# A post-norm decoder layer in 8-bit arithmetic: the order of a batch's maximum and the next batch's norm on VectorE

## The chip, the cores and the metric

The kernel runs on one core of a Trainium2 chip. The core has a matrix engine (TensorE, PE in the profile), a vector engine (VectorE, DVE), a scalar engine (ScalarE, ACT), GpSimd (POOL), and SyncE (SP), which here only issues transfers. Sixteen DMA engines move data between HBM and SBUF. The engines run their own instruction streams in order and meet through semaphores. The metric is the time of one execution on the device in microseconds, given as the median of several runs.

## The reference

The program computes three blocks of a decoder, each followed by a residual add and a layer norm: a self-attention whose activations and weights pass through power-of-two 8-bit quantisers, a cross-attention in f32, and a feed-forward block with quantised weights and a low-rank addition. x is (8, 512, 512), the context is (8, 512, 384), and there are 16 heads. What matters here is the start of the self-attention:

```python
def _pot_scale(x):
    m = jnp.maximum(jnp.max(jnp.abs(x)), 1e-08)
    return jnp.exp2(jnp.ceil(jnp.log2(m / INT8_MAX)))

mu = jnp.mean(x, axis=-1, keepdims=True)
var = jnp.var(x, axis=-1, keepdims=True)
h = (x - mu) * jax.lax.rsqrt(var + LN_EPS)
h = h * fq_round(ln_gamma) + fq_round(ln_beta)
qkv = fq_floor(fq_floor(h) @ fq_round(w_qkv))
```

The scale of fq_floor(h) is one number for all eight batches. It needs the largest absolute value of h over the whole tensor, so no value of h can be quantised before the last batch has been normed, and no product of h can start before that.

## The kernel before, in words

The work is cut into stages, each between places where all five engines meet. The change lies in the first stage (from the start to the first product with w_qkv, 0 to 153.16 us in the profiled execution). A batch is 512 tokens by 512 features; it is held as four tiles of 128 tokens.

For each batch b of the first stage:

- **SyncE** (lines 434 to 461) loads x of batch b into one of two buffers `xB[:, b % 2]` (1 MB) and the context into one of two buffers `cx[:, b % 2]`. For b + 2 it may only do so when the buffer is free: x waits for `z_turned` of batch b, the context for `kv_mm` of batch b. Then it waits for `h_ready` of batch b and stores h to `h_scr` (1 MB). All of these go down one queue in this order. ScalarE issues the loads of w_qkv and w_out (8.4 MB) on a queue of its own, once x of batches 0 and 1 is in (lines 1276 to 1280).
- **VectorE** runs `first_norm(b)` (lines 1601 to 1607): a wait for x, four `bn_stats` (L1573), four `bn_aggr` (L1579), twelve small steps for the reciprocal root (L1582 to L1590), and four 128x512 multiply-subtracts in place (L1598), each of which raises `z_ready`.
- **TensorE** turns the context (`turn_ctx`, L843, 12 transposes), then z (`turn_z`, L833, 16 transposes). `turn_z(b)` waits for `h_ready` of batch b - 1, since z of all batches is turned into the same four banks, and for `z_ready` of each tile.
- **ScalarE** takes the turned context out of its banks (L1294), then applies gamma and beta on the way out of the banks of z (`h_out`, L1288, four of 128x512), raises `h_ready`, and writes into one of two buffers `hB[:, b % 2]`. For b of 2 and more it first waits until h of batch b - 2 is stored and until its maximum is taken (`h_peak` at b - 1).
- **VectorE** runs `h_peak(b)` (lines 1618 to 1620): a wait for `h_ready` of batch b, then one reduction over 128x2048 (L1516 `stats<-arena`).

VectorE also does one-off work, put between the batches: the maximum of w_qkv and w_out (`weight_peaks`, b = 2, L1516 `peak<-arena`), their scales (b = 3), and their quantisation (L1633, L1634 at b = 3 and 4; L1637, L1638 at b = 5). After the maximum of the last batch it folds the eight maxima, GpSimd reduces over the partitions, VectorE makes the scale, SyncE's reload of h from `h_scr` must have landed, and `quantise_h` (L1665, L1669) makes the first operand of stage two, whose matmuls are L855.

The order on VectorE is the order in which the program text calls these functions; nothing reorders them. The loop of lines 1640 to 1654 writes it out.

Of the kernel before, what the change touches and what calls it, by code (L numbers as in the profile page):

```python
# [73 lines left out]
def decoder(nc, x, ctx_768, g_ln, b_ln, w_qkv, w_out, log_temp, Wq, bq, Wk, bk, Wv, bv, Wo, bo,  # L74
# [20 lines left out]
    with ExitStack() as ctx:  # L95
# [80 lines left out]
        def S(name):  # L176

            if name not in names:
                names[name] = sem(name)
            return names[name]  # L180
# [1324 lines left out]
        def _(dve):  # L1505
# [9 lines left out]
            def amax(dst, src, ax=AX.X):  # L1515
                return V.tensor_reduce(dst, src, ax, ALU.max, apply_absolute_value=True)  # L1516
# [75 lines left out]
            def norm_stats(ch, src):  # L1592

                norm_moments(ch, src)
                norm_factors(ch)

            def normed(dst, src, t):
                return V.tensor_scalar(dst, src, mv[:, t, 0:1], rstd[:, t:t + 1], ALU.subtract, ALU.mult)  # L1598


            def first_norm(b):
                ch = Chain(dve, S("norm_step"), NORM, b)
                dve.wait_ge(S(f"x_in{b % 2}"), 16 * (b // 2) + 16)
                norm_stats(ch, xB[:, b % 2])
                for t in range(NT):
                    normed(xB[:, b % 2, t, :], xB[:, b % 2, t, :], t).then_inc(S("z_ready"), 1)
                ch.end()

            def gamma_beta():
                dve.wait_ge(apeak_ready, 1)  # L1610
                power_of_two(S_GAMMA, S_BETA + 1)
                for n, (v, k) in enumerate(((gam, S_GAMMA), (bet, S_BETA))):
                    g8 = gam8[:, KC * n:KC * n + KC]
                    link(V.tensor_scalar(g8, v[:, :], iv(k), None, ALU.mult))
                    link(V.tensor_scalar(v[:, :], g8, sc(k), None, ALU.mult))
                dve.sem_inc(S("b16_ready"), 1)

            def h_peak(b):
                dve.wait_ge(S("h_ready"), b * KC + KC)
                amax(stats[:, b:b + 1], hB[:, b % 2], AX.XY).then_inc(S("h_peak"), 1)  # L1620

            def weight_peaks():
                dve.wait_ge(S("wA_in"), 16 * (KC + 1))
                link(amax(peak[:, S_WQKV:S_WQKV + 1], wqkv_f, AX.XY))
                link(amax(peak[:, S_WOUT:S_WOUT + 1], wout_f, AX.XY))
                dve.sem_inc(peak_ready, 1)

            def weight_scales():
                dve.wait_ge(apeak_ready, 2)
                power_of_two(S_WQKV, S_WOUT + 1)  # L1630

            def quantise_wqkv(k):
                link(V.tensor_scalar(w8[:, 0:3 * INNER], wqkv_f[:, k, :], iv(S_WQKV), None, ALU.mult))  # L1633
                link(V.tensor_copy(wqkv_q[:, k, :], w8[:, 0:3 * INNER]))  # L1634

            def quantise_wout():
                link(V.tensor_scalar(w8[:, :], wout_f.rearrange("p a b -> p (a b)"), iv(S_WOUT), None, ALU.mult))  # L1637
                link(V.tensor_copy(wout_q.rearrange("p a b -> p (a b)"), w8[:, :]))  # L1638

            first_norm(0)  # L1640
            gamma_beta()
            for b in range(NB - 1):
                h_peak(b)
                first_norm(b + 1)
                if b == 2:
                    weight_peaks()
                if b == 3:
                    weight_scales()
                if b in (3, 4):
                    quantise_wqkv(2 * b - 6)  # L1650
                    quantise_wqkv(2 * b - 5)
                if b == 5:
                    quantise_wout()
# [499 lines left out]
```

## Time and profile before

| | us |
|---|---|
| median of 3 runs | 2945.56 |
| lowest and highest of them | 2941.08, 2950.68 |
| the profiled execution, its own time | 2947.2 |
| its span, first to last instruction | 2945.4 |
| TensorE busy, VectorE busy, ScalarE busy | 2549.4, 2387.9, 1403.5 |
| first product of stage two starts at | 153.16 |

How to read the rows below. A row of the timeline has the start in us from the start of the span, the duration, the engine, the line, the operation with output and input, the count, and in brackets the idle time of this engine just ahead of it with what ended that idle time. A row of the waits has the engine and line that waited, what it waited for, the total in us, the times, and the longest. SPq and ACTq rows are transfers being issued, at their start. An issue row of the transfers has the size and the us from issue to landing; each such row comes from a stretch of time with that one issue in it. A row of a stretch of time has its bounds and length, then busy us and count of PE, PEld (weight loads), DVE, ACT and POOL, TensorE's granted clock as a share of 2.4 GHz, the DMA share, and GB/s.

### The profile page before, as it was taken

The numbers are of one execution on the slowest core, as the hardware profiler recorded it, in microseconds if no ns is written. First come the engines' busy times: TensorE is split into PE (matmuls) and PEld (weight loads), VectorE is DVE, ScalarE is ACT, GpSimd is POOL, SyncE is SP. The second block draws the span as 40 slices with busy tenths as digits, with TensorE's granted clock in tenths as the row PEclk, the third lists the DMA queues.
The fourth block names the chain that finished last, engine by engine and source line by source line (L and its number), as shares of the span: only waits on it lengthen the run. The fifth ranks groups of instructions, "written<-read, shape, count | busy, mean of one in ns | idle before, by whom it ended". The sixth has DMA issues, their size and how long they took to land.

```text
span 2945.4 us, 43234 instructions
## 1 busy us (share of the span) xinstructions
PE 2549.4 (87%) x13176; PEld 995.6 (34%) x13176; DVE 2387.9 (81%) x4130; ACT 1403.5 (48%) x2456; POOL 217.9 (7%) x210
## 2 busy tenths in 40 slices
PE   3299899969999957777769799999999999999997
PEld 3244322212222224444335222222223444444443
DVE  7889499999999969999889589988897755555554
ACT  2200233318998989999523155555555322221211
POOL 0000233310111110000000000111100000000000
PEclk7599999969998979999989899999999999999999
DMA  8342222214454543443216633443355510000000
GB/s 320 109 184 93 90 105 101 94 65 158 164 180 150 164 144 113 128 125 114 72 43 200 152 84 102 115 110 103 101 169 197 197 72 29 29 29 28 29 29 29
DMA packets 197749, 332.90 MB, mean 113 GB/s; under 512 B 32504, under 2 KB 118520, under 8 KB 187248
## 3 DMA queue, kind: packets, MB, share of 16 engines
q1 hardware_dynamic: 193312, 314.51, 33.2%
q10 hardware_dynamic: 4304, 16.78, 1.5%
q8 instruction: 63, 1.03, 0.1%
q14 instruction: 70, 0.57, 0.1%
HBM read 200.70 MB, written 130.51 MB: 112 GB/s over the span
## 4 chain that ended last, share of the span: by engine, by line
PE 53%; DVE 21%; issue 15%; ACT 7%; DMA 2%; DVEq 1%; SPq 0%; POOLq 0%; POOL 0%; ACTq 0%
PE bank L1068 9%; PE bank L1234 7%; PE bank L1223 7%; ACT arena L1329 6%; DVE stats L1516 6%; PE bank L1024 4%; DVE arena L1797 4%; PE bank L1032 4%; PE bank L1008 4%; PE bank L1122 3%; DVE arena L1812 3%; PE bank L915 2%; PE bank L923 1%; PE bank L1040 1%; PE bank L983 1%
## 5 line engine op out<-in xcount | busy, mean ns | idle before, releaser
L1516 DVE TENSOR_REDUCE stats<-bank 128x1024 f32 (+1 forms) x352 | 406.4, 1216 | 54.8 <-PE bank L892 32.4
L1329 ACT ACTIVATE arena<-arena 128x512 bf16<-128x512 int8 x512 | 361.4, 713 | 72.9 <-DVE arena L1733 72.8
L1750 DVE CUSTOM_DVE_ANT_0 arena<-bank,arena,fac 128x512 int8<-128x512 f32 x512 | 355.8, 740 | 20.7 <-PE bank L915 20.7
L1917 DVE TENSOR_REDUCE arena<-bank 128x2 f32<-128x1024 f32 x256 | 312.5, 1223 | 52.1 <-PE bank L1024 36.4
L1422 ACT ACTIVATE arena<-bank 128x1024 f32<-128x1024 f32 x256 | 248.0, 1022 | 189.4 <-PE bank L1040 189.4
L1354 ACT ACTIVATE arena<-arena 128x512 f32<-128x512 int8 x512 | 323.7, 774 | 14.6 <-DMA arena<-dq_scr 14.6
L1492 ACT ACTIVATE arena<-bank,bf_s,fac 128x512 f32<-128x512 f32 x128 | 99.5, 778 | 434.1 <-PE bank L1226 434.1
L1307 ACT ACTIVATE arena<-bank,floor_c,fac 128x1024 int8<-128x1024 f32 x96 | 115.6, 1204 | 355.2 <-PE bank L855 304.6
L1068 PE MATMUL bank<-arena 128*32 128x512 f32 x2048 | 270.0, 604 | 0.0
L855 PE MATMUL bank<-arena 128*128 128x512 bf16 x1024 | 245.4, 384 | 26.3 <-DMA arena<-hq_scr 13.2
L1234 PE MATMUL bank<-arena 128*128 128x512 f16 x1024 | 245.6, 379 | 7.6 <-DVE arena L2114 7.1
L1223 PE MATMUL bank<-arena 128*128 128x512 f16 x1024 | 243.1, 380 | 0.0
L2084 DVE TENSOR_SCALAR arena<-arena 128x512 f16<-128x512 f32 x128 | 54.6, 426 | 228.0 <-ACT arena L1492 226.5
L949 PE MATMUL bank<-identb,arena 128*128 128x128 bf16 x2048 | 138.2, 221 | 83.6 <-DVE arena L1812 79.0
L915 PE MATMUL bank<-arena 64*128 64x512 bf16 x512 | 169.4, 400 | 36.2 <-DVE arena L1750 24.9
L1024 PE MATMUL bank<-arena 128*128 128x512 f16 x512 | 157.6, 391 | 19.8 <-DMA arena<-half_scr 13.0
L1812 DVE TENSOR_SCALAR arena<-arena,inv 128x2048 bf16<-128x2048 f32 x128 | 164.0, 1281 | 13.0 <-ACT arena L1354 10.8
L1943 DVE TENSOR_SCALAR arena<-arena 128x1024 f32<-128x1024 f32 (+1 forms) x192 | 166.0, 865 | 5.1 <-ACT arena L1422 5.1
L949 PEld LDWEIGHTS bank<-identb,arena 128*128 128x128 bf16 x2048 | 116.1, 98 | 145.2 <-DVE arena L1812 107.0
L1797 DVE TENSOR_SCALAR arena<-bank 128x2048 bf16<-128x2048 bf16 x128 | 155.7, 1217 | 0.0
L1032 PE MATMUL bank<-arena 128*128 128x512 f16 x512 | 155.3, 387 | 0.4
L960 PE MATMUL bank<-arena 128*64 128x512 bf16 x512 | 131.9, 379 | 23.8 <-DVE arena L1797 23.2
(211 smaller groups left out, 3397.3 us busy)
## 6 DMA issues: line engine op xcount, KB each, us to landing
dq_scr<-arena SPq DMA_DIRECT2D x128, 256.0 KB, 2.1
arena<-dq_scr SPq DMA_DIRECT2D x128, 256.0 KB, 2.6
arena<-half_scr SPq DMA_DIRECT2D x256, 128.0 KB, 2.8
qkv_scr<-arena SPq DMA_DIRECT2D x8, 3072.0 KB, 9.7
arena<-in_x SPq DMA_DIRECT2D x16, 1024.0 KB, 8.4
arena<-qkv_scr SPq DMA_DIRECT2D x128, 128.0 KB, 2.4
half_scr<-arena SPq DMA_DIRECT2D x32, 512.0 KB, 4.0
x_scr<-arena SPq DMA_DIRECT2D x16, 1024.0 KB, 5.7
```

Source lines behind the costliest of these rows:

```text
L949: last = nc.tensor.transpose(PT[s % 2][:, j, P * t:P * t + P], aG[:, s % 2, t, P * j:P * j + P], identb[:, :])
L1024: last = mm(bank[:, at + t % 2, :], Qs[:, r, hs, P * t:P * t + P], Ks[:, r, hs, :], start=True, stop=True)
L1032: mm(bank[:, 2 + g, :], Ks[:, r, g, P * c:P * c + P], Qs[:, r, g, :], start=True, stop=False)
L1068: last = mm(bank[XD * g:XD * g + XD, 7 if k < 2 else 6, :], w, eT[:, par, g, c, :], start=c == 0, stop=c == NT - 1)
L1223: mm(dst, Wf[:, k, P * s:P * s + P], xx[:, par, k, :], start=k == 0 and n == 0, stop=False)
L1234: last = mm(bank[:, t, :], gg[:, f % 8, P * t:P * t + P], Wp[:, f, :], start=f == 0 and n == 0, stop=False)
L1329: last = A(e_dump[:, NT * (h % 2) + t, :], dq8[:, h % 4, t, :], ACT.Exp, bias=negm_b[:, par, c:c + 1], scale=exp_scale, accum_out=sum_b[:, ...
L1354: A(eG[:, s % 2, t, :], dqG[:, s % 4, t, :], ACT.Exp, bias=negm_g[:, par, c:c + 1], scale=exp_scale).then_inc(S("eG_done"), 1)
L1516: return V.tensor_reduce(dst, src, ax, ALU.max, apply_absolute_value=True)
L1750: V.tensor_tensor_reduce(dq8[:, s, t, :], bank[:, t, :], floor_row, fac[:, C_DOTS:C_DOTS + 1], -3.0e38, ALU.add, ALU.max, accum_out=ymax[: ...
L1797: V.tensor_scalar(aTG[:, h % 2].rearrange("p a b -> p (a b)"), PT[h % 2].rearrange("p a b -> p (a b)"), -129.0, None, ALU.add).then_inc(S( ...
L1917: V.tensor_reduce(mxX[:, mp, hs, 2 * u:2 * u + 2], bank[:, at:at + 2, :], AX.X, ALU.max).then_inc(S("sX_red"), 1)
```

## The change

In the loop over the batches `first_norm(b + 1)` now stands ahead of `h_peak(b)`. Nothing else is edited.

```diff
             for b in range(NB - 1):
+                first_norm(b + 1)
                 h_peak(b)
-                first_norm(b + 1)
                 if b == 2:
                     weight_peaks()
```

VectorE's instruction stream changes in the first stage alone; those of the other four engines are the same. Here is VectorE just behind the quantised gamma and beta (the row on L1615), before. `stats<-arena` is the maximum of h, `bn6`, `mv` belong to the norm.

```order
45 L1615 TENSOR_SCALAR bet<-gam8,scale 128x4
46 L1516 TENSOR_REDUCE stats<-arena 128x1
47 L1573 BN_STATS bn6<-arena 128x6 x4
48 L1579 BN_AGGR mv<-bn6 128x2 x4
49 L1582 TENSOR_SCALAR var_eps<-mv 128x4
```

The same place in the changed kernel, and the end of this norm (rows 49 to 58 are its small steps):

```order
45 L1615 TENSOR_SCALAR bet<-gam8,scale 128x4
46 L1573 BN_STATS bn6<-arena 128x6 x4
47 L1579 BN_AGGR mv<-bn6 128x2 x4
48 L1582 TENSOR_SCALAR var_eps<-mv 128x4
...
59 L1590 SCALAR_TENSOR_TENSOR rstd<-newton,rstd 128x4
60 L1598 TENSOR_SCALAR arena<-arena,mv,rstd 128x512 x4
61 L1516 TENSOR_REDUCE stats<-arena 128x1
62 L1573 BN_STATS bn6<-arena 128x6 x4
```

The norm of batch 1 moved ahead of the maximum of batch 0, and the norm of batch 2 follows that maximum.

The second place is VectorE around the quantisation of w_out (L1637, L1638), the last one-off work. Before, the maximum of batch 6 (row 161) stands between it and the norm of batch 7 (row 162 on), and the maximum of batch 7 (row 177) follows that norm:

```order
158 L1598 TENSOR_SCALAR arena<-arena,mv,rstd 128x512 x4
159 L1637 TENSOR_SCALAR arena<-arena,inv 128x4096
160 L1638 CAST arena<-arena 128x4096
161 L1516 TENSOR_REDUCE stats<-arena 128x1
162 L1573 BN_STATS bn6<-arena 128x6 x4
...
176 L1598 TENSOR_SCALAR arena<-arena,mv,rstd 128x512 x4
177 L1516 TENSOR_REDUCE stats<-arena 128x1
178 L1516 TENSOR_REDUCE peak<-stats 128x1
```

Now the maximum of batch 5 (row 158) stands ahead of that work, the norm of batch 7 follows it at once, and the maxima of batches 6 and 7 stand behind that norm:

```order
157 L1598 TENSOR_SCALAR arena<-arena,mv,rstd 128x512 x4
158 L1516 TENSOR_REDUCE stats<-arena 128x1
159 L1637 TENSOR_SCALAR arena<-arena,inv 128x4096
160 L1638 CAST arena<-arena 128x4096
161 L1573 BN_STATS bn6<-arena 128x6 x4
...
175 L1598 TENSOR_SCALAR arena<-arena,mv,rstd 128x512 x4
176 L1516 TENSOR_REDUCE stats<-arena 128x1 x2
177 L1516 TENSOR_REDUCE peak<-stats 128x1
```

One maximum fewer stands ahead of the norm of batch 7, and one more behind it.

## Rows read from the trace of the kernel before

**Rows 1.** Waits of VectorE, 20 to 152 us.
```profile
DVE stats L1516 <- ACT arena L1288: 18.0, 5, 5.3
DVE arena L1665 <- DMA arena<-h_scr: 2.7, 1, 2.7
```

**Rows 2.** Timeline of VectorE, first stage.
```profile
20.04 0.23 DVE L1615 TENSOR_SCALAR bet<-gam,scale 128x4 f32<-128x4 int8 x1
23.18 2.29 DVE L1516 TENSOR_REDUCE stats<-arena 128x1 f32<-128x2048 f32 x1 [2.91 <-ACT arena L1288]
...
37.98 2.29 DVE L1516 TENSOR_REDUCE stats<-arena 128x1 f32<-128x2048 f32 x1 [5.28 <-ACT arena L1288]
...
51.61 2.29 DVE L1516 TENSOR_REDUCE stats<-arena 128x1 f32<-128x2048 f32 x1 [4.11 <-ACT arena L1288]
53.81 2.46 DVE L1573 BATCH_NORM_STATS2 bn<-arena 128x6 f32<-128x512 f32 x4
...
61.04 17.39 DVE L1516 TENSOR_REDUCE peak<-arena 128x1 f32<-128x12288 f32 x2
...
128.54 2.29 DVE L1516 TENSOR_REDUCE stats<-arena 128x1 f32<-128x2048 f32 x1 [0.76 <-ACT arena L1288]
130.74 2.46 DVE L1573 BATCH_NORM_STATS2 bn<-arena 128x6 f32<-128x512 f32 x4
...
143.01 2.29 DVE L1516 TENSOR_REDUCE stats<-arena 128x1 f32<-128x2048 f32 x1 [4.94 <-ACT arena L1288]
```

**Rows 3.** Timeline of TensorE, first stage.
```profile
31.48 3.65 PE L833 MATMUL bank<-ident,arena 128*128 128x128 f32 x16 [9.96 <-DVE arena L1598]
40.78 2.82 PE L843 MATMUL bank<-ident,arena 128*128 128x128 f32 x12 [5.66 <-DMA arena<-in_ctx]
46.28 2.48 PE L833 MATMUL bank<-ident,arena 128*128 128x128 f32 x16 [2.67 <-DVE arena L1598]
...
136.84 3.32 PE L833 MATMUL bank<-ident,arena 128*128 128x128 f32 x16 [9.66 <-DVE arena L1598]
```

**Rows 4.** Timeline of ScalarE, first stage: weight loads issued, h of batch 1.
```profile
13.35 1.94 ACTq L1279 DMA_DIRECT2D arena<-in_L_attn_w_qkv  x4
...
35.16 2.78 ACT L1288 ACTIVATE arena<-bank,bet,gam 128x512 f32<-128x512 f32 x4 [10.56 <-PE bank L833]
```

**Rows 5.** Timeline of SyncE's issues, first stage.
```profile
20.11 0.37 SPq L430 DMA_DIRECT2D arena<-in_x  x1
...
23.18 0.34 SPq L454 DMA_DIRECT2D h_scr<-arena  x1
35.16 0.37 SPq L430 DMA_DIRECT2D arena<-in_x  x1
...
37.97 2.14 SPq L454 DMA_DIRECT2D h_scr<-arena  x1
...
143.44 1.32 SPq L442 DMA_DIRECT2D arena<-h_scr  x2
```

**Rows 6.** Issue to landing: w_out, then the first four issues of rows 5, in order.
```profile
arena<-in_L_attn_w_out ACTq DMA_DIRECT2D x1, 2048.0 KB, 30.8
...
arena<-in_x SPq DMA_DIRECT2D x1, 1024.0 KB, 15.9
...
h_scr<-arena SPq DMA_DIRECT2D x1, 1024.0 KB, 20.7
...
arena<-in_x SPq DMA_DIRECT2D x1, 1024.0 KB, 12.8
...
h_scr<-arena SPq DMA_DIRECT2D x1, 1024.0 KB, 14.4
```

**Rows 7.** Three stretches of time at the start of stage two.
```profile
153.00:155.00 2.00, 1.84 (x5) 0.73 (x6) 0.03 (x1) 0.00 (x0) 0.00 (x0) 0.50 0.57 215
155.00:157.00 2.00, 2.00 (x7) 0.70 (x5) 0.21 (x1) 0.00 (x0) 0.00 (x0) 0.56 0.98 285
157.00:159.00 2.00, 2.00 (x11) 0.88 (x9) 1.44 (x2) 0.00 (x0) 0.00 (x0) 1.00 1.02 397
```

## Prediction, made before the changed kernel ran

> **What bounds the kernel now.** I read the first stage alone, since only VectorE's stream there changes. First the waits [rows 1]: behind the first norm, between 20 and 152 us, VectorE waits 18.0 us in five pieces, each time in front of the maximum of a batch's h, for ScalarE. The one other wait of size, 2.7 us, comes at the end, for h being read back. Then the timeline [rows 2]: the five pieces are 2.91, 5.28, 4.11, 0.76 and 4.94 us, which sum to 18.0, so there is no sixth. Between 61.04 and 128 us nothing is waited for but the 0.76. VectorE is the engine that sets this stage's end: each piece is the round trip in which z of a batch is turned on TensorE (3.65 us) and taken out by ScalarE (2.78 us) while VectorE, whose next instruction is that batch's maximum, stands still [rows 3, 4]. The norm of the next batch, which needs only x, stands behind the maximum.
>
> Last the transfers, because the norm moves ahead into a time in which they are slow. SyncE issues x of batch 2 at 20.11 and it lands 15.9 us later, at 36.0; h of batch 0 lands at 23.18 + 20.7 = 43.9; x of batch 3 at 35.16 + 12.8 = 47.96; h of batch 1 at 37.97 + 14.4 = 52.4 [rows 5, 6]. The context of batch 2 lets TensorE go at 40.78 [rows 3]. They are slow because w_qkv and w_out were issued from 13.35 us on [rows 4]. Before the change both x were there when asked for; now they would be asked for earlier.
>
> **The change part by part.** Nothing is added or removed. Each maximum costs 2.20 us from its start to the start of the norm behind it (51.61 to 53.81), each norm 7.23 us (53.81 to 61.04) [rows 2]. The sum is made by running the new order with these two durations.
>
> Batch 1. The last step on beta ends at 20.27 [rows 2], x of batch 1 is in (ScalarE's loads, which wait for it, go at 13.35 [rows 4]). The norm runs from 20.3 to 27.5, the maximum of batch 0, ready at 23.18, to 29.7.
>
> Batch 2. x lands at 36.0, and its issue doesn't move, since it waits for batch 0's z. So VectorE waits 6.3 us, a new wait in place of old ones. The norm ends at 43.2. The maximum of batch 1 is long ready: its z is now turned from 20.3 + 6.1 = 26.4 on, where 6.1 is the time from a norm's start to the first transposition (130.74 to 136.84 [rows 2, 3]), and h comes 3.65 + 2.8 us later, at 32.9. That maximum ends at 45.4.
>
> Batch 3. x of batch 3 is now issued when z of batch 1 has been turned, at 30.1 instead of 35.16. I take its landing as unchanged, 47.96: it stands in the same queue behind x and context of batch 2 and h of batch 0, and the last of those still lands at 43.9, since the 20.11 and the 23.18 don't move. So VectorE waits 2.5 us. The norm ends at 55.2. The maximum of batch 2 needs h of batch 2, and there TensorE is held by the context: 40.78 + 2.82 = 43.6, then z 2.48 us, then ScalarE 2.8 us, 48.9 [rows 3, 4]. That is covered by 6 us. The maximum ends at 57.4, and the maxima of the weights start there instead of at 61.04: **3.6 us ahead**. Both weights are in by then: w_out, the last of them, is issued at 13.35 + 1.94 = 15.3 us and lands 30.8 us later, at 46.1 [rows 4, 6].
>
> The middle. From the weights' maxima to the start of the norm of batch 7 before it took 130.74 - 61.04 = 69.70 us. The new order has the same work in it less one maximum (that of batch 6, now behind the norm of batch 7), 2.20 us, and less the wait of 0.76 in front of it: 66.74. Every other maximum in the middle now has a whole norm more for its h to come, so no wait can be new. The norm of batch 7 starts at 57.4 + 66.7 = 124.1 instead of 130.74: **6.6 us ahead**, 3.6 from the start and 3.0 from here.
>
> The end. From the norm of batch 7 to its h took 143.01 - 130.74 = 12.27 us: norm, transposition, ScalarE. No maximum shortens it. It now also covers the maximum of batch 6: VectorE is done with both at 124.1 + 7.23 + 2.3 = 133.6 and waits 2.8 us for h at 136.4. So of the old 4.94 us there, some 2.8 stay. What is late next is this round trip itself. Behind it all is unchanged and shifts with it: the fold, GpSimd, the scale, and the reload of h, which SyncE issues 0.43 us after batch 7's h is ready and for which VectorE waits 2.7 us [rows 1, 5]. The h buffers cost nothing: ScalarE needs the maximum of batch b - 2 before it writes h of batch b, and on VectorE that maximum still stands ahead of the norm of batch b, without which there is no z.
>
> The sum: new waits 6.3 + 2.5 + 2.8 = 11.6 us against 18.0 before, a gain of 6.4; by start times 143.01 - 136.4 = 6.6. I take 6.6. The profiled execution has 2947.2 us with a span of 2945.4, so its time would become 2940.6. The median of the three runs is 2945.56, 1.6 lower, so the prediction for a median is 2945.56 - 6.6 = 2939.0. That is 0.22%. A measurement of this kernel can tell about 0.3% (8.8 us) from no change, so the likeliest case is a gain that is real but counts as no difference.
>
> The unknown term is the landing of x of batches 2 and 3 in a queue that now fills sooner. Bounds from rows: x of batch 3 can't land later than 52.4, when all that the queue held up to h of batch 1 has landed [rows 5, 6], whatever order the bytes take. The weights' maxima would then start at 52.4 + 9.4 = 61.8, 0.8 later than before, and the gain is 3.0 - 0.8 = 2.2. If x of batch 2 is slowed for the 5.9 us in which it shares with the newly issued transfers, to 42 us, and x of batch 3 is on time, they start at 42 + 2 x 9.43 = 60.9 and the gain is 3.1. If x of batch 3 comes as early as it is wanted (45.4), they start at 36.0 + 2 x 9.43 = 54.9, and the gain is 6.1 + 3.0 = 9.1. I take the unchanged landing, as the rows show landings in the order of issue: 36.0, 43.9, 47.96, 52.4. The duration of one z turned varies too, 2.48 to 3.65 us against the 3.32 of batch 7 [rows 3]: 0.8 more or 0.3 less.
>
> The Trainium skill's page "DMA: Bandwidth & Descriptors", section "Queues, rings and completion order", speaks against that choice: descriptors start in ring order on each DMA engine, but completion is "not FIFO per issuing engine". By the ring order alone the sum would be 6.6; by the loose completion it could be anything down to 2.2. The trace of before agrees with the first, since these four landings are in order.
>
> **The rivals.**
>
> *The queue serves the new issues at the old ones' cost.* A second wait then takes the old one's place: x of batch 2 or 3 comes late. For it: the transfers of batch 1 are issued 5 us sooner while everything is slow. Against it: the order of landings [rows 6]. Gain 2.2 to 3.1, time 2942.5 to 2943.4.
>
> *x of batch 3 comes sooner because it is asked for sooner.* Gain up to 9.1, time 2936.5. Against it: the queue was never empty between 20.11 and 47.96, so asking sooner doesn't bring the turn sooner.
>
> *The transfers don't matter and all waits in front of the maxima vanish but the last.* Three batches at 9.43 from 20.3 on put the weights' maxima at 48.6, gain 12.4 + 3.0 = 15.4, time 2930.2. Against it: x of batch 2 at 36.0 is from a row, and nothing moves its issue.
>
> *The gain is not on the path, or the order does not free VectorE.* Stage two would have to wait for something else that doesn't shift. For it I find nothing but the reload of h (2.7 us), which hangs on the same h of batch 7. Time 2945.6.
>
> *Slower: TensorE's clock in stage two.* At its start the granted clock is 0.50 (1.2 GHz), with 5 matmuls in 2 us; by 157 us it is 1.00 (2.4 GHz), with 11 in 2 us [rows 7]. TensorE has been idle since it turned batch 7. One matmul costs 0.40 us at the low level (2 us by 5) and 0.18 at the high one, 0.22 more. If the rise came later in the new phase, the point from which this decides is 6.6 / 0.22 = 30 more matmuls at the low level; if the whole first batch of stage two (32 units of 4 matmuls, 128) ran low it would cost 28 us, and the time would be 2939.0 + 28 = 2967. For it: in the first stage bursts of 16 transpositions run at the low level to their end (3.65 us). Against it: the clock rose after about ten matmuls in this place, and the idle time ahead of them, the round trip behind batch 7, keeps its length.
>
> On this last rival the Trainium skill ("TensorE: Matmul & The Clock Gate", "What's actually happening") says that the default state is throttled and activity releases it. By that the same matmuls release it as soon as before, and this rival would give 2939.0.
>
> **How the numbers follow.** Chances: forecast 0.68; x of batch 2 or 3 late 0.12; x of batch 3 sooner 0.06; all waits gone 0.04; gain lost 0.05; slower 0.05. The range: from a gain of 9.1 to one of 2.2 the time is 2936.5 to 2943.4, and the three runs shown lie 4.5 below and 5.1 above their median, of which a median of a few runs takes perhaps the larger half; so 2932 to 2947. Faster by over 0.3% (under 2936.7): a quarter of the forecast's 0.68, since its 6.6 is 2.2 short of the bound and the spread of runs is wider than that, plus half of the 0.06, plus the 0.04, together 0.25. Slower by over 0.3%: 0.05. Within: 0.70.
>
> **What would show each step.** In the timeline of VectorE after: the first norm behind beta starts at 20.3; the norm of batch 2 has an idle time of some 6 us ahead of it ended by the DMA of x, that of batch 3 one of some 2.5; the weights' maxima start at 57.4; between them and the end no wait is left; the last maximum has some 2.8 us of waiting for ScalarE and starts at 136.4; the first product of stage two starts at 146.6. If the weights' maxima start at 60 or later, the queue was at fault; if at 49 to 55, x landed sooner than I say. If stage two starts at 146.6 and the span doesn't follow, the loss lies behind it, and the granted clock or a later stage must show it.

## The result, and the profile after

The changed kernel takes 2938.61 us in the median (18 runs, 2925.04 to 2944.7), the kernel before 2945.74 in as many runs of its own (2937.91 to 2953.28). The medians lie 7.1 us apart, and the ratio is 0.9975 with a 95% interval of 0.9966 to 0.9985: a gain clear of no change, and under the 0.3% that the prediction took as what a measurement can tell. The profiled execution has 2941.5 us with a span of 2939.7.

The timeline of VectorE in the first stage, after, answers rows 2:

```profile
20.27 0.23 DVE L1615 TENSOR_SCALAR bet<-gam,scale 128x4 f32<-128x4 int8 x1
20.66 2.47 DVE L1573 BATCH_NORM_STATS2 bn<-arena 128x6 f32<-128x512 f32 x4 [0.15 <-DVE bet L1615]
...
27.90 2.28 DVE L1516 TENSOR_REDUCE stats<-arena 128x1 f32<-128x2048 f32 x1
35.40 2.47 DVE L1573 BATCH_NORM_STATS2 bn<-arena 128x6 f32<-128x512 f32 x4 [5.22 <-DMA arena<-in_x]
...
42.65 2.27 DVE L1516 TENSOR_REDUCE stats<-arena 128x1 f32<-128x2048 f32 x1
47.51 2.47 DVE L1573 BATCH_NORM_STATS2 bn<-arena 128x6 f32<-128x512 f32 x4 [2.59 <-DMA arena<-in_x]
...
56.95 17.40 DVE L1516 TENSOR_REDUCE peak<-arena 128x1 f32<-128x12288 f32 x2
...
123.73 2.47 DVE L1573 BATCH_NORM_STATS2 bn<-arena 128x6 f32<-128x512 f32 x4
...
130.98 2.28 DVE L1516 TENSOR_REDUCE stats<-arena 128x1 f32<-128x2048 f32 x1
136.20 2.29 DVE L1516 TENSOR_REDUCE stats<-arena 128x1 f32<-128x2048 f32 x1 [2.95 <-ACT arena L1288]
...
143.65 1.29 DVE L1665 TENSOR_SCALAR arena<-arena,inv 128x2048 int8<-128x2048 f32 x1 [2.71 <-DMA arena<-h_scr]
```

The maxima (`stats<-arena`) no longer have idle time ahead of them, but for the last. Two norms (L1573) have it instead, ended by the transfer of x. The waits of VectorE, 20 to 147 us, answer rows 1: 18.0 us behind ScalarE have become 2.9, and 7.8 behind x are new.

```profile
DVE bn L1573 <- DMA arena<-in_x: 7.8, 2, 5.2
DVE stats L1516 <- ACT arena L1288: 2.9, 1, 2.9
DVE arena L1665 <- DMA arena<-h_scr: 2.7, 1, 2.7
```

TensorE turns z of batch 1 at once behind its norm, and z of batch 2 behind the context (compare rows 3):

```profile
26.76 3.65 PE L833 MATMUL bank<-ident,arena 128*128 128x128 f32 x16 [5.01 <-DVE arena L1598]
40.25 2.82 PE L843 MATMUL bank<-ident,arena 128*128 128x128 f32 x12 [9.84 <-DMA arena<-in_ctx]
42.87 2.63 PE L833 MATMUL bank<-ident,arena 128*128 128x128 f32 x16
```

And SyncE's issues of x of batches 2 and 3 with their time to landing (compare rows 5 and 6):

```profile
20.35 0.37 SPq L430 DMA_DIRECT2D arena<-in_x  x1
...
30.44 0.37 SPq L430 DMA_DIRECT2D arena<-in_x  x1
```

```profile
arena<-in_x SPq DMA_DIRECT2D x1, 1024.0 KB, 15.0
...
arena<-in_x SPq DMA_DIRECT2D x1, 1024.0 KB, 17.0
```

x of batch 3 is issued 4.7 us sooner than before and lands at 47.4 instead of 47.96: it takes 17.0 us where it took 12.8.

**The measure for the experiments.** The first quantisation of h (L1665 above) is the end of the first stage on VectorE. It starts at 150.48 before and at 143.65 after, 6.8 us sooner. From there to the end of the span the time is 2794.9 us before and 2796.1 after. So nothing of the gain lies behind the first stage in these two traces; the 1.1 us more there is well inside the scatter of that part (10.7 us, told at the end). I use this start in all runs. The first product of stage two is a poorer mark: the timeline shows it at 146.74 after, with 62 of the 64 matmuls that stood there before, and 1.77 us behind the start of the cast on L1669 (144.97) instead of 1.36 (151.80 to 153.16), so its first two records are missing in that trace. The same holds for e1_end, e2_start and e3_late, where stage two is shown some 0.4 us late.

### The profile page after: what moved, and what is told of

Same layout as the page of the kernel before. It is cut to its first block, busy times and chain, and to the rows that moved or that the text cites. A ratio compares the mean times of both kernels' runs of the same rounds, so it can differ in the third digit from the quotient of the medians.

```text
span 2939.7 us, 43186 instructions
## 1 busy us (share of the span) xinstructions
PE 2541.5 (86%) x13128; PEld 995.2 (34%) x13176; DVE 2388.3 (81%) x4130; ACT 1403.5 (48%) x2456; POOL 213.4 (7%) x210
## 4 chain that ended last, share of the span: by engine, by line
PE 53%; DVE 21%; issue 14%; ACT 7%; DMA 3%; DVEq 1%; SPq 0%; POOLq 0%; POOL 0%; ACTq 0%
PE bank L1068 9%; PE bank L1234 7%; PE bank L1223 7%; ACT arena L1329 6%; DVE stats L1516 5%; PE bank L1024 4%; DVE arena L1797 4%; PE bank L1032 4%; PE bank L1008 4%; PE bank L1122 3%; DVE arena L1812 3%; PE bank L915 2%; PE bank L923 1%; PE bank L1040 1%; PE bank L983 1%
## 5 line engine op out<-in xcount | busy, mean ns | idle before, releaser
L2084 DVE TENSOR_SCALAR arena<-arena 128x512 f16<-128x512 f32 x128 | 54.5, 426 | 227.1 <-ACT arena L1492 225.6
L960 PE MATMUL bank<-arena 128*64 128x512 bf16 x512 | 131.1, 377 | 23.9 <-DVE arena L1797 23.3
```

## The experiments

Each was compared with the kernel before on the same chip. "First quantisation" is its start on VectorE in the one trace of each run; before it is 150.48. e3_late and e4_before_late ran once, so their total times say nothing here. Two traces differ by up to about 1 us in this start without any cause in the edit (see e1_end), so smaller differences are not read.

| run | what it is | first quantisation | gain | ratio of the whole, 95% |
|---|---|---|---|---|
| changed kernel | | 143.65 | 6.8 | 0.9975, 0.9966 to 0.9985 |
| e1_end | the end's reorder alone | 148.86 | 1.6 | 0.9996, 0.9979 to 1.0012 |
| e2_start | the start's reorder alone | 146.08 | 4.4 | 0.9979, 0.9963 to 0.9994 |
| e3_late | changed, weights later | 148.18 | 2.3 | one run |
| e4_before_late | before, weights later | 155.56 | -5.1 | one run |
| e5_hidden | changed, w_out's work at the end | 138.29 | 12.2 | 0.9966, 0.995 to 0.9982 |
| e8_reload | changed, early reload | 144.04 | 6.4 | 0.9971, 0.9956 to 0.9985 |
| e12_store | e8_reload, store wait split | 140.35 | 10.1 | 0.9956, 0.9941 to 0.9971 |
| e10_fill | changed, w_qkv's maximum in the waits | 136.00 | 14.5 | 0.9967, 0.9951 to 0.9984 |
| e11_fill_before | before, the same filling | 143.93 | 6.6 | 0.999, 0.9973 to 1.0006 |
| e9_best | changed, with fill, hidden and store | 128.98 | 21.5 | 0.9933, 0.9913 to 0.9953 |

### The two parts of the gain, one at a time

e1_end moves only the maximum of batch 6:

```diff
+                if b == NB - 2:
+                    first_norm(b + 1)
                 h_peak(b)
-                first_norm(b + 1)
+                if b < NB - 2:
+                    first_norm(b + 1)
```

e2_start has the same with `b < 3` and `b >= 3`, and so moves only the maxima of batches 0 to 2.

> Only the last maximum moves: the maximum of batch 6 stands behind the norm of batch 7, the order of batches 0 to 5 is that of the kernel before. Theory (the gain has two separate parts, 3.6 us in front of the maxima of the weights, where the landing of x takes over as the limit, and 3.0 us at the end): the maxima of the weights start at 61.0 us as before, the norm of batch 7 starts 3.0 us earlier (2.2 for the maximum that no longer stands ahead of it, 0.8 for the wait in front of it), and the first product of stage two starts at 150.2 instead of 153.2; total 3 us less. Rival (there is one pool of waiting, which the end alone can win back or can't touch): stage two starts at 146.7 or at 153.2.

Measured, VectorE's timeline of e1_end:

```profile
52.56 2.29 DVE L1516 TENSOR_REDUCE stats<-arena 128x1 f32<-128x2048 f32 x1 [5.28 <-ACT arena L1288]
...
61.99 17.41 DVE L1516 TENSOR_REDUCE peak<-arena 128x1 f32<-128x12288 f32 x2
...
128.79 2.47 DVE L1573 BATCH_NORM_STATS2 bn<-arena 128x6 f32<-128x512 f32 x4
...
141.41 2.29 DVE L1516 TENSOR_REDUCE stats<-arena 128x1 f32<-128x2048 f32 x1 [3.08 <-ACT arena L1288]
```

The moved work did what was said: from the weights' maxima to the norm of batch 7 it is 66.80 us, against 69.70 before and 66.74 predicted. But the gain at the first quantisation is only 1.6, and stage two starts at 151.95 (with 62 records) instead of the expected 150.2. The weights' maxima started 0.95 us late, at 61.99, since the third maximum waited 5.28 us instead of 4.11 [rows 2]: z of batch 2 took 3.65 us to turn in this execution at a granted clock of 0.50, and 2.48 in that of before [rows 3] at 0.75. The last round trip, 12.62 us instead of 12.27, took 0.35 more for the same reason: its 16 transpositions took 3.65 us at 0.50, 3.32 at 0.57 before. So the 3.0 of the end is right, and on top of it lies a scatter of about 1 us by which clock a burst of transpositions gets. The rival's numbers (146.7 or 153.2) didn't come out, but this run's 1.6 us alone wouldn't tell 3 from nothing; the 66.80 does.

> Only the maxima of batches 0 to 2 stand behind the next norm; from batch 3 on the order is that of the kernel before. Theory: VectorE waits for x of batch 2 (5 to 6 us) and of batch 3 (2.5 us) as in the changed kernel, the maxima of the weights start at 57.0 to 57.4 us, nothing is gained later, the last maximum waits 4.9 us as before, and stage two starts at 149.2 to 149.6; total 3.6 to 4.1 us less than before. Rival (a gain at the start is given back in the middle, since the maximum of batch 3 comes earlier there and its h may be late): stage two starts at 153.2.

Measured, waits of VectorE in e2_start and two rows of its timeline:

```profile
DVE bn L1573 <- DMA arena<-in_x: 7.3, 2, 5.6
DVE stats L1516 <- ACT arena L1288: 6.0, 2, 5.3
```

```profile
56.27 17.39 DVE L1516 TENSOR_REDUCE peak<-arena 128x1 f32<-128x12288 f32 x2
...
146.08 1.29 DVE L1668 TENSOR_SCALAR arena<-arena,inv 128x2048 int8<-128x2048 f32 x1 [2.73 <-DMA arena<-h_scr]
```

The weights' maxima start 4.8 us sooner than before, and the first quantisation 4.4 us. The start's gain is carried through the middle and is not given back; the last maximum waits 5.3 us, like a full round trip in the old order. I had given 57.0 to 57.4 for the weights' maxima, and they start at 56.27, since x of batch 3 landed sooner than in the changed kernel's trace (46.8 against 47.4). Stage two is shown at 149.17 (149.2 to 149.6 expected), also with 62 records. The two parts together (4.4, and 1.6 with the 0.95 it lost at its start) make 7.0, against the 6.8 of the changed kernel.

### What the new wait for x is

e3_late and e4_before_late issue the weights' loads from ScalarE behind its work on batch 0 and take their maxima one batch later:

```diff
-            for par in (0, 1):
-                act.wait_ge(S(f"x_in{par}"), 16)
-            for k in range(KC):
-                act.dma_start(wqkv_f[:, k, :], chunk(w_qkv)[:, k, :]).then_inc(S("wA_in"), 16)
...
+                if b == 0:
+                    load_weights()
...
-                if b == 2:
+                if b == 3:
                     weight_peaks()
```

> The changed order, but ScalarE issues the loads of w_qkv and w_out only after it has taken out h of batch 0 (about 23.3 us instead of 13.35), and the maxima of the weights come one batch later (after batch 3), their scales and quantisation of w_qkv at batches 4 and 5. Theory (the new wait for x of batch 2 is the traffic of the weights): x of batch 2 lands 6 to 8 us after its issue, before 29 us, and VectorE doesn't wait for it; x of batch 3 is now issued into the traffic of the weights, so a wait of 0 to 8 us comes back there. Stage two starts between 139 and 147. Rival (x lands late whatever else is moved, because of the queue it is in): the wait of 5 us in front of the norm of batch 2 stays.

Measured, VectorE in e3_late, then its two busy DMA queues from 28 to 36 us and from 44 to 52 us (q1 is SyncE's, q10 ScalarE's; columns are packets, MB, share of 16 engines):

```profile
29.82 2.46 DVE L1574 BATCH_NORM_STATS2 bn<-arena 128x6 f32<-128x512 f32 x4
51.64 2.47 DVE L1574 BATCH_NORM_STATS2 bn<-arena 128x6 f32<-128x512 f32 x4 [12.31 <-DMA arena<-in_x]
```

```profile
q10 hardware_dynamic: 272, 2.95, 87.4%
q1 hardware_dynamic: 270, 0.41, 14.1%
```

```profile
q1 hardware_dynamic: 746, 1.61, 52.5%
q10 hardware_dynamic: 755, 1.55, 50.8%
```

The wait in front of the norm of batch 2 (29.82) is gone, as the theory said, so it is the traffic of the weights: x of batch 2 landed 5.5 us after its issue, not 15.0. The other half of the expectation was wrong: I gave the wait in front of batch 3 at most 8 us, and it is 12.3; the first quantisation came at 148.18, later than in the changed kernel, and stage two at 151.3, outside the 139 to 147 I gave. x of batch 3, issued at 30.02, took 21.6 us. The queue rows say why. The two queues move packet for packet, 272 against 270; but ScalarE's, which are w_qkv, are 10.8 KB in the mean and SyncE's 1.5 KB, so SyncE's queue gets one seventh of what the weights get while w_qkv is under way. 1.5 KB is one row of the context (384 f32). So what moves there is the context of batch 2, issued at 20.25 and landed at 41.9. In the same queue behind it h of batch 0 landed at 45.9 and then x of batch 3 at 51.6. With w_out (2 KB packets) the shares become equal.

x of batch 2 had met the same in the kernel before. Here are the two queues from 24 to 28 us there, SyncE's with packets of 2 KB, which is a row of x (512 f32):

```profile
q10 hardware_dynamic: 122, 1.30, 81.7%
q1 hardware_dynamic: 119, 0.24, 18.6%
```

The weights are 8.4 MB wherever they are put; x of batch 3 lands at 47.4 with the weights issued from 13.35 on and at 51.6 with those issued from 20.3 on. (They went out at 20.3 and not at the 23.3 I wrote, since the issue on ScalarE didn't wait for the arithmetic ahead of it: it stands at 20.32 in the trace, and the last of the four activations that precede it in the program began at 22.31.)

> The order of the kernel before, with the loads of the weights and their maxima moved as in the run before this one. Theory (in the old order VectorE stands still for the round trip through TensorE and ScalarE, not for transfers): the waits in front of the maxima of batches 1 to 3 are about 5 us each, one more such wait than before since the maximum of batch 3 is no longer covered by those of the weights, and stage two starts at 157 to 159 us, 4 to 5 later than before. Rival (the old waits too come from the traffic of the weights): the waits shrink and stage two starts before 153.

Measured, the waits of VectorE in e4_before_late:

```profile
DVE stats L1517 <- ACT arena L1287: 23.0, 5, 5.3
```

23.0 us where the old order had 18.0: a round trip of 5.27 is new, in front of the maximum of batch 3, the 0.76 is gone, and the others are as long as before or up to 0.35 us longer. The first quantisation comes 5.1 us later, and stage two starts at 158.65 (157 to 159 expected). The weights are not out of the way for all of it: they were issued from 20.28 on and had landed by 54.5. But the waits in front of the maxima of batches 3 and 7, at 66.5 and 148.1 us, come after that and are 5.27 and 5.28 us long. So the waits of the old order are the round trip through TensorE and ScalarE, and those of the new order are transfers.

The pair shows one thing more. x of batch 3 was issued at 35.06 here and took 16.8 us, so it landed at 51.9; in e3_late it was issued at 30.02, 5.0 us sooner, and landed at 51.6. When it is asked for makes next to no difference to its landing; when the weights are issued does.

### Filling the new waits

e10_fill and e11_fill_before take the maximum of w_qkv in four pieces, in the new and in the old order (the four loads of w_qkv raise semaphores of their own):

```diff
+            def piece_peak(k):
+                link(amax(stats[:, PIECE + k:PIECE + k + 1], wqkv_f[:, k, :]))
...
                 h_peak(b)
+                if b == 0:
+                    piece_peak(0)
+                    piece_peak(1)
+                if b == 1:
+                    piece_peak(2)
```

> The changed kernel, with the maximum of w_qkv taken in pieces where VectorE waits for x: two of its four parts (6.5 us) between the maximum of batch 0 and the norm of batch 2, one (3.2 us) ahead of the norm of batch 3, the last with w_out in the old place. Theory (the waits of 5.2 and 2.6 us for x of batches 2 and 3 are free time on VectorE): both waits go, the norm of batch 4 starts at 66.4 instead of 74.5, stage two starts at 138.6, 8 us sooner than in the changed kernel; total 2931 against 2946 before. Rival (the landing of x of batch 3 moves back with the z of batch 1 or with the slower drain of the queue): the wait in front of the norm of batch 3 stays near 2.6 us.

Measured, VectorE in e10_fill:

```profile
36.29 2.47 DVE L1573 BATCH_NORM_STATS2 bn<-arena 128x6 f32<-128x512 f32 x4
49.11 2.47 DVE L1573 BATCH_NORM_STATS2 bn<-arena 128x6 f32<-128x512 f32 x4
...
136.00 1.29 DVE L1678 TENSOR_SCALAR arena<-arena,inv 128x2048 int8<-128x2048 f32 x1 [2.69 <-DMA arena<-h_scr]
```

Both norms start with no idle time ahead of them, 0.9 and 1.6 us later than in the changed kernel, with about 10 us of work done in between. The first quantisation is 7.65 us sooner than there. Stage two was given at 138.6 and is at 138.69. The total came to 2935.4, not the 2931 I gave: 10.2 us less than the kernel before. The ratio's interval reaches to about the 14.5 us of the first stage, so whether all of them arrive in the total isn't shown.

> The order of the kernel before, with the maximum of w_qkv in pieces as in the run before this one (6.5 us ahead of the maximum of batch 1, 3.2 us ahead of that of batch 2). Theory (the waits in front of the maxima are idle time of VectorE, which work can fill in either order; reordering and filling draw on the same waits at the start, but not at the end): the wait of 5.3 us in front of the maximum of batch 1 goes, that in front of batch 2 falls by 3.2 us, and stage two starts at 144 to 146 us; without the reordering it lacks the 3 us of the end and what of the start isn't filled, so it ends later than the filled changed kernel by about 6 us. Rival (filling makes the reordering superfluous): stage two starts within 1 us of the run before.

Measured in e11_fill_before:

```profile
54.05 2.29 DVE L1516 TENSOR_REDUCE stats<-arena 128x1 f32<-128x2048 f32 x1 [2.09 <-ACT arena L1288]
...
143.93 1.29 DVE L1678 TENSOR_SCALAR arena<-arena,inv 128x2048 int8<-128x2048 f32 x1 [2.91 <-DMA arena<-h_scr]
```

The old order is filled too, with 2.1 us left in front of batch 2, and gains 6.6 us; stage two starts at 146.61, a little outside the 144 to 146 I gave. It ends 7.9 us behind the filled new order (6 were expected). Filling doesn't make the reorder superfluous.

### What is left at the end

> The changed kernel, with the quantisation of w_out taken out from between the maximum of batch 5 and the norm of batch 7: its first step (2.3 us) stands between the maxima of batches 6 and 7, its second (2.3 us) behind the scale of h, where VectorE waits 2.7 us for h to be read back. Theory (behind the norm of batch 7 the round trip through TensorE and ScalarE sets the end, and VectorE has 3 us of room in it and 2.7 us in the reload): the norm of batch 7 starts 4.7 us sooner than in the changed kernel, at 119.1, the last maximum at 131.5, the wait in front of it shrinks from 2.9 to about 0.6 us, and stage two starts at 142.1. Rival (those waits are not room but traffic or the like): stage two stays at 146.7.

e5_hidden takes `quantise_wout()` out of the loop, its first step behind `h_peak(6)`, its second behind the scale of h. Measured:

```profile
130.88 2.29 DVE L1516 TENSOR_REDUCE stats<-arena 128x1 f32<-128x2048 f32 x1 [0.64 <-ACT arena L1288]
...
138.29 1.29 DVE L1667 TENSOR_SCALAR arena<-arena,inv 128x2048 int8<-128x2048 f32 x1 [0.33 <-DMA arena<-h_scr]
```

The wait in front of the last maximum is 0.64 us (0.6 expected), that for the reload 0.33, and the first quantisation is 5.4 us sooner than in the changed kernel: 4.7 of hidden work (56.36 to 118.46 from the weights' maxima to the norm of batch 7, 62.10 us instead of 66.78), and 0.6 of scatter at the start (the weights' maxima at 56.36 instead of 56.95). Stage two starts at 140.97, 1.1 us sooner than the 142.1 I gave. The two waits were room.

> The changed kernel, with SyncE issuing the reload of h of batches 0 and 1 ahead of its wait for h of batch 7 instead of behind it. The reload then goes out when z of batch 7 has been turned, about 133.4 us, instead of 136.6. Theory (the 2.7 us wait behind the scale is the transfer itself, 7 us from its issue): it lands at 140.4, before the scale is ready, the wait is gone and stage two starts at 144.0 to 144.4. Rival (the landing is set by the store of h of batch 7 that now goes beside it): the wait stays and stage two starts at 146.7.

e8_reload puts SyncE's reload of h of batches 0 and 1 ahead of its wait for h of batch 7 and of its store. Measured, VectorE, and the landing of the store of h of batch 7, issued at 135.64:

```profile
144.04 1.29 DVE L1665 TENSOR_SCALAR arena<-arena,inv 128x2048 int8<-128x2048 f32 x1 [3.65 <-DMA h_scr<-arena]
```

```profile
h_scr<-arena SPq DMA_DIRECT2D x1, 1024.0 KB, 8.2
```

Nothing was gained, and the theory was wrong: a wait for a transfer of 2.7 us became one of 3.65, with another releaser, and stage two starts at 146.72. That is the rival, to the number. VectorE's code waits for both stores and the reload ahead of the quantisation, and the store now shared the engines with the reload and landed last, at 143.84, 8.2 us after its issue instead of the 4.8 of the changed kernel. (The weights' maxima started 0.7 us sooner in this trace than in the changed kernel's; counted from them, the first quantisation comes 1.1 us later.)

> The run with the early reload (e8_reload), and VectorE waits for the store of h of the even batches alone before the first quantisation of h, for that of the odd ones behind it. In e8_reload the wait in front of that quantisation was 3.65 us, ended by the store of h of batch 7, which was issued at 135.6 and took 8.2 us beside the reload. Theory (the store's landing took the reload's place as the last of two conditions, and the reload itself was in time): the first quantisation starts at 140.4 or earlier, the wait is under 0.5 us, stage two starts at 143.0 to 143.5. Rival (the reload lands as late as the store, since both share the queue): the wait stays at 3 us or more and stage two starts near 146.7.

```diff
-            for n in (0, 1):
-                dve.wait_ge(S(f"h_stored{n}"), 16 * NB // 2)
+            dve.wait_ge(S("h_stored0"), 16 * NB // 2)
             quantise_h(0, 0)
+            dve.wait_ge(S("h_stored1"), 16 * NB // 2)
```

The first quantisation writes only over the buffer of the even batches' h, so the store of batch 7 needn't be waited for. Measured in e12_store:

```profile
140.35 1.28 DVE L1665 TENSOR_SCALAR arena<-arena,inv 128x2048 int8<-128x2048 f32 x1
```

No wait is left ahead of it, it starts 3.7 us sooner than in e8_reload, and stage two starts at 143.04 (143.0 to 143.5 expected). The reload had been in time in both; the store was the whole of the 3.65 us.

### All of it

> The changed kernel with all three: the maxima of w_qkv in pieces in the waits for x (e10_fill), w_out's quantisation behind the norm of batch 7 (its second step behind the first quantisation of h, where VectorE waits 3.8 us for TensorE), and the early reload with the split wait for the stores (e12_store). Theory (each takes a different wait, so they add): the norm of batch 4 starts at 66.7, that of batch 7 at 111.3, the last maximum at 123.8, stage two at 131.0 to 131.5, 22 us before the 153.2 of the kernel before; total 0.992 to 0.993 of it. Rival (one uses up what another needs, e.g. the reload lands after the scale since the norm of batch 7 comes sooner): stage two at 134 or later.

```profile
DVE stats L1516 <- ACT arena L1288: 0.9, 1, 0.9
```

```profile
124.21 2.29 DVE L1516 TENSOR_REDUCE stats<-arena 128x1 f32<-128x2048 f32 x1 [0.90 <-ACT arena L1288]
...
128.98 1.29 DVE L1679 TENSOR_SCALAR arena<-arena,inv 128x2048 int8<-128x2048 f32 x1
```

0.9 us is what is left in e9_best of the 18.0 that VectorE waited for ScalarE. The last maximum starts at 124.21 (123.8 expected), and stage two at 131.67 (131.0 to 131.5). They add: the first quantisation is 21.5 us sooner than before, where the changed kernel's 6.8 and what e10_fill (7.7), e5_hidden (5.4) and e12_store (3.3) had on top of it sum to 23.1; the 1.6 between them is about what the scatter of single traces would make, and no run tells it apart from a small overlap. The median is 2927.1 against 2946.12, the ratio 0.9933 (0.9913 to 0.9953). That is clear of the kernel before. Its interval also lies wholly below the changed kernel's (0.9966 to 0.9985), though the two were not run side by side.

## Why the prediction was right

Point by point, predicted and measured, in us:

| step | predicted | measured |
|---|---|---|
| norm of batch 1 starts | 20.3 | 20.66 |
| wait for x of batch 2, norm starts | 6.3, 36.0 | 5.22, 35.40 |
| wait for x of batch 3, norm starts | 2.5, 47.96 | 2.59, 47.51 |
| maxima of the weights start | 57.4 | 56.95 |
| from there to the norm of batch 7 | 66.74 | 66.78 |
| wait ahead of the last maximum, its start | 2.8, 136.4 | 2.95, 136.20 |
| gain of the first stage | 6.6 | 6.8 |
| median | 2939.0 | 2938.6 |

**The mechanism** was right: VectorE stood still for a round trip, the next norm was work it could do in that time, and the landing of x took over as the limit. The step that decides the size, x of batch 3 landing where it did though issued sooner, held to 0.5 us (47.96 and 47.4). It holds beyond this one trace: the old order has it at 46.5 in e1_end and 47.0 in e11_fill_before, and the new one at 46.8 in e2_start and e8_reload, 46.9 in e5_hidden and 47.1 in e12_store, though the new order issues it 4 to 5 us sooner. e3_late and e4_before_late show that the one kind of wait is transfers and the other is not.

**How much of the agreement is luck.** The parts came to 4.1 at the start (3.6 predicted), 2.9 in the middle (3.0), and 0.2 lost in the last round trip (0), together 6.8. The median fell within 0.4 us of the forecast, while the interval of the ratio is some 3 us wide to either side: that closeness is chance, the sign and the size are not.

**The landing's reason** was only half told. I argued by the order in the queue, and the landings bear that out: they came in order of issue, and x of batch 3 landed behind the context of batch 2 and h of batch 0 before, after and in e3_late. What the argument left open is what sets the queue's pace. That is how much of the weights goes through beside it, packet for packet. Asked sooner, x waited longer. No run puts x ahead of the context or of the store, so how much the order alone is worth isn't shown. The Trainium skill's sentence that completion is not in order within one issuer ("DMA: Bandwidth & Descriptors", "Queues, rings and completion order") had been weighed against this. Nothing came of it here: the changed kernel's transfers landed at 35.35 (x of batch 2), 40.2 (context), 43.6 (h of batch 0) and 47.4 (x of batch 3), in their order of issue. In the same section the Trainium skill says that each engine takes turns between the queues with work, a whole packet at a time. The equal packet counts of e3_late agree; whether a packet of the profile is what the skill calls one, no run shows.

**The rivals.** x late (2942.5 and more): the landing was on time. x sooner or all waits gone: no, 7.8 us remained. Gain lost behind the first stage: 2794.9 and 2796.1 us behind it, no loss beyond the scatter of runs. Slower by TensorE's clock at the start of stage two: no. In the changed kernel the granted clock there is 0.50, 0.51 and 1.00 in three stretches of 2 us from 146.17 on, against 0.50, 0.56 and 1.00 before [rows 7]. The premise that bursts of transpositions run low to their end holds only for most of them: the same rows 3 have one of 2.48 us.

**The chances.** The gain is 0.25%, with an interval of 0.15 to 0.34%, "within 0.3%" as the likeliest case had it. (The terms given for "faster" sum to 0.24, not 0.25.) The scatter that made me give 0.25 to faster is real: the time behind the first quantisation differed between the twelve profiled executions from 2788.6 (e3_late) to 2799.3 us (e8_reload), 10.7 us, in kernels whose code there is the same but for the second step of w_out in e9_best and a few waits. That is more than the change is worth. What makes it is open. The mean granted clock was 0.949 in the first of these and 0.943 in the second, but 0.948 in e9_best, which had 2799.0, so the clock alone doesn't order them.

## What to carry to other kernels

When an engine's in-order stream waits for a round trip through other engines, put work behind its next independent step, and run the new order through the landing times of what that step reads: the wait moves to the next input in line, and its size can be read from the trace before. Work that sits between the last steps of a stage belongs in the waits that are left (w_qkv's maximum, w_out's quantisation); with an earlier reload and a split wait for the stores it was worth 14.7 us on top here, more than the reorder itself. When a wait covers several conditions, removing the last one to arrive shows the next: look at the releaser, not only at the length.

## What the runs showed of the hardware

Two DMA queues that both had work shared the sixteen engines packet for packet in the stretches read here (272 against 270 in 8 us of e3_late, 755 against 746 in another 8, 122 against 119 in 4 us before), with equal packets and with unequal ones. So a load with 10.8 KB packets took 87% of the engines' time and one with 1.5 KB packets 14%; against 2 KB packets it was 82% and 19%. Here the stream of large packets held back the more urgent one of small packets: 1 MB of x took 15.9 us beside the weights and 5.5 with the weights issued later.

The burst of 16 transpositions of batch 2 took 1.97 us in e5_hidden at a mean granted clock of 0.98 of 2.4 GHz, 2.48 before at 0.75, 2.63 after at 0.72, and 3.65 in e1_end at 0.50, that is 1.2 GHz to its end. Where such a burst lies on a round trip that an engine waits for, an otherwise exact sum has about 1 us of scatter.
